# One GNN layer pair on one core: the factor pieces on ScalarE's queue, the destination rows behind the table stores, the order test ahead of the node scales

## The chip, the cores and the metric

The kernel runs on one core of one Trainium2 chip. Time is device microseconds of that core. The kernel before takes 2129.64 us (median of three runs, 2129.09 to 2132.87). The execution that the profiler recorded took 2125.4 us by its own clock, of which the profile's span covers 2123.5 us.

## The reference

6250 nodes with 512 features each, 100000 edges sorted by destination. Two Chebyshev graph convolutions stand around a layer norm, ahead of them a layer norm with ReLU, and at the end the input is added again:

```python
deg  = segment_sum(ones(E), src, N)
dinv = where(deg > 0, rsqrt(maximum(deg, 1.0)), 0.0)
norm = -dinv[src] * dinv[dst]

def prop(h):                       # one sum over the edges of each node
    return segment_sum(h[src] * norm[:, None], dst, N)
def cheb_conv(h, W0, W1, b):
    return h @ W0 + prop(h) @ W1 + b

h = relu(layernorm(x))
h = cheb_conv(h, W1_0, W1_1, b1)
h = layer_norm(h, gamma, beta)
h = where(h >= 0, h, 0.01 * h)
out = x + cheb_conv(h, W2_0, W2_1, b2)
```

## The kernel before, in words

The work has a setup and two layers.

**Setup.** SyncE's queue (SP in the profile) loads the edge sources and then all of x into `arena`, as 125 partitions of 50 nodes each, in eleven groups of tiles, every group in a piece of 112 and one of 13 partitions (L339). ScalarE (ACT) makes sum, squares and ReLU of most tiles (L536 to L555), VectorE (DVE) those of eight tiles. VectorE also builds one-hot tiles of the edge sources (L787) and TensorE (PE) multiplies them into a histogram, which is the degree of every node (L1107). The normalized rows go to a table in HBM, `table[0]`, whose rows have 516 elements: 512 features and behind them a factor of the node (four elements, 16 bytes, of which the first is used). SP stores the features, group by group, in twenty DMAs (L359, semaphore `s_tab`, shown as table0_out). The factor needs the degrees, so it is ready last: VectorE's reciprocal at L832 raises `s_factor`. It is stored in three pieces, each a DMA of as many 16-byte runs as it has nodes: 48 partitions from ScalarE's queue (L574, 2400 runs), 64 and 13 partitions from SP's (L363, 3200 and 650 runs). All three raise `s_factor_out` (row_factors_out).

**Edges.** The edges are cut into 782 columns of 128, called slots, and 53 chunks of 14 or 15 slots; a chunk sums into 128 nodes from a base. For that the kernel needs the source index of every slot (`idx_all`) and its destination (`dst_rows`, turned into `loc_all`). SP loads both as rows (`slot_rows`, L343 to L347, three DMAs each) ahead of the table stores; TensorE turns them (`turn`, L1100). VectorE writes `idx_all` (L850), casts the destinations (L853), tests that the edges are sorted (`order`, L734 to L743), works out the chunks' bases (`bases`, L750 to L782, which raises `s_flag` and `s_base`), and makes `loc_all` ready (L861 to L883, `s_loc`). The scales of the nodes (L833 to L844, `s_scales`) stand ahead of all this, right behind the factor. SP stores them (L365), loads the first weights (L368, 2 MB) and then the first chunk's own rows and scales (L375, L377).

**Layers.** GpSimd (POOL) issues one indirect DMA per slot (L494), which gathers 128 rows of the table into one of 30 row buffers: 782 in each layer, 1564 in all. In layer 0 it has to wait for the whole table, `s_tab` and `s_factor_out`. ScalarE rounds a gathered row (L597, L598) into PSUM and SBUF, VectorE makes the remainder (L918, L922) and one-hot tiles (L892, L893), TensorE multiplies one-hots with rows (L1221 to L1230) and does the dense parts (L1093). A buffer is free when the slot is summed: GpSimd waits for `s_slot` of two chunks before, every five slots. Layer 1 does the same from `table[1]`, which layer 0 writes.

What sets the order around the change: each engine's program is written out by hand; a queue takes its DMAs in the order of the program. GpSimd's program waits for `idx_all`, the flag, the table and the factors, and then branches to `general` (edges not sorted) or `layer` (sorted, the case here):

```python
pool.wait_ge(s_idxr, 2)
pool.wait_ge(s_flag, 1)
bad = pool.value_load(flag_i[0:1, 0:1], min_val=0, max_val=1)
pool.wait_ge(s_tab, 2 * 16 * (NG - 1))
pool.wait_ge(s_factor_out, 48)
with pool.If(bad > 0):
```

Of the kernel before, what the change touches and what calls it, by code (L numbers as in the profile page):

```python
# [14 lines left out]
P = 128  # L15
# [18 lines left out]
def gnn_kernel(nc, x, src, dst, W10, W11, b1, gamma, beta, W20, W21, b2, out):  # L34
    N, D = x.shape
# [6 lines left out]
    TA = 112  # L42
    ACT_ROWS = 48

# [49 lines left out]
    with ctx:  # L94
# [234 lines left out]
        def _(sp):  # L329
# [21 lines left out]
            slot_rows(src, idx_all, s_idx)  # L351
            slot_rows(dst, dst_rows, s_dsts)
            for g in range(1, NG):
# [4 lines left out]
                for n0, n1 in parts:  # L358
                    sp.dma_start(table_rows[n0:n1, t0:t1, 0:D], nodes[n0:n1, t0:t1, :]).then_inc(s_tab, 16)  # L359
            sp.wait_ge(s_factor, 1)  # L360
            with nc.allow_non_contiguous_dma(reason="the factor in each row of the table"):
                for n0, n1 in ((ACT_ROWS, TA), (TA, TR)):
                    sp.dma_start(table_rows[n0:n1, :, D:RW], factors[n0:n1, :, :]).then_inc(s_factor_out, 16)  # L363
            sp.wait_ge(s_scales, 1)
# [89 lines left out]
        def _(pool):  # L454
# [9 lines left out]
            def general(L):  # L464
                if L == 1:
                    pool.wait_ge(s_gout, 16 * (NC + 1))
                with pool.Fori(0, NC) as i:
                    n = L * NC + i
# [15 lines left out]
            def layer(L):  # L484
                if L == 1:
                    pool.wait_ge(s_tab1, 16 * (NC + 1))
                for i in range(NC):
                    u = i % 2
# [12 lines left out]
            bad = pool.value_load(flag_i[0:1, 0:1], min_val=0, max_val=1)  # L501
            pool.wait_ge(s_tab, 2 * 16 * (NG - 1))
            pool.wait_ge(s_factor_out, 48)
            with pool.If(bad > 0):
# [7 lines left out]
        def _(act):  # L512
# [60 lines left out]
            with nc.allow_non_contiguous_dma(reason="the factor in each row of the table"):  # L573
                act.dma_start(table[0].rearrange("(p t) n -> p t n", t=NT)[0:ACT_ROWS, :, D:RW],  # L574
                              factors[0:ACT_ROWS, :, :]).then_inc(s_factor_out, 16)

# [115 lines left out]
        def _(dve):  # L692
# [117 lines left out]
            for t in range(HT):  # L810
# [7 lines left out]
                if mine is not None:  # L818
# [12 lines left out]
            dve.wait_ge(s_sqvdeg, 1)  # L831
            nc.vector.reciprocal(factors[:, :, 0], sqrt_veps_deg).then_inc(s_factor, 1)  # L832
            post.add(nc.vector.tensor_scalar(hasdeg, hist_ps[0:TR, 0:NT], 0.0, None, ALU.is_gt))  # L833
            dve.wait_ge(s_sqdeg, 2)
# [12 lines left out]


            dve.wait_ge(s_idxps, 1)
            nc.vector.tensor_copy(idx_all[:, 0:4 * P], src_ps[0][:, :]).then_inc(s_idxr, 1)  # L850
            nc.vector.tensor_copy(idx_all[:, 4 * P:S], src_ps[1][:, 0:S - 4 * P]).then_inc(s_idxr, 1)
            dve.wait_ge(s_dsts, 48)
            nc.vector.tensor_copy(dst_rows_f[:, 0:FB * P], dst_rows[:, 0:FB * P]).then_inc(s_dstrows, 1)  # L853
            nc.vector.tensor_copy(dst_rows_f[0:S - FB * P, FB * P:],
                                  dst_rows[0:S - FB * P, FB * P:]).then_inc(s_dstrows, 1)

            order()
            bases()

# [225 lines left out]
        def _(pe):  # L1085
# [11 lines left out]
            def turn(to, source):  # L1097
                for b in range(FB + 1):
                    n = min(P, S - b * P)
                    last = nc.tensor.transpose(to[b // 4][:, b % 4 * P:b % 4 * P + n], source[0:n, b * P:(b + 1) * P],  # L1100
                                               ident[0:n, 0:n])
                return last
# [10 lines left out]
            with pe.Fori(0, HT // 2) as k:  # L1113
# [8 lines left out]

            pe.wait_ge(s_dstrows, 2)
            turn(dst_ps, dst_rows_f).then_inc(s_locps, 1)
            pe.wait_ge(s_viol, 1)
# [3 lines left out]
            nc.tensor.matmul(misc_ps[:, 192:192 + NC], ones_row[:, :], chunk_f[:, 0, :], start=True,  # L1129
                             stop=True).then_inc(s_basesum, 1)  # L1130
            pe.wait_ge(s_flag, 1)
            bad = pe.value_load(flag_i[0:1, 0:1], min_val=0, max_val=1)
# [162 lines left out]
```

## Time and profile before

| | |
|---|---|
| median of three runs | 2129.64 us (2129.09 to 2132.87) |
| the profiled execution | 2125.4 us |
| its span | 2123.5 us |
| first gather starts | 113.58 us |
| gathers | 1564 |
| PE busy | 1900.1 us (89%) |
| ACT busy | 1509.1 us (71%) |
| POOL busy | 1487.0 us (70%) |
| DVE busy | 1457.6 us (69%) |

The busy shares are averages over the whole span. GpSimd's 70% leaves out the time between two of its instructions, which is not counted as busy. The setup is the first 113.6 us; ScalarE works without a gap in it until 94.9 us, and the DMA engines are busy until about 107 us. "SPq" and "ACTq" rows are the DMA instructions of those queues: their duration is the time that the issuing engine needs to hand over the DMA, not the transfer.

### The profile page before, as it was taken

How to read it: one execution, taken by the hardware profiler on the slowest of the kernel's cores; microseconds unless marked ns; L12 is line 12 of the kernel's file. 1: busy time of each engine (PE TensorE's matmuls, PEld its weight loads, DVE VectorE, ACT ScalarE, POOL GpSimd, SP SyncE). 2: the span in 40 equal slices, each digit the busy share in tenths (PEclk: the TensorE clock that was granted, in tenths of full speed). 3: DMA queues.
4: the chain of work that ended last, by engine and by line, in shares of the span. 5: the costliest groups of instructions: out<-in, count | busy, mean ns of one | idle time of the engine just before them, and what ended most of it. 6: DMA issues, size and time to landing. Idle time of an engine off the chain costs nothing.

```text
span 2123.5 us, 25622 instructions
## 1 busy us (share of the span) xinstructions
PE 1900.1 (89%) x6702; PEld 1067.5 (50%) x6702; DVE 1457.6 (69%) x3379; ACT 1509.1 (71%) x2720; POOL 1487.0 (70%) x1574
## 2 busy tenths in 40 slices
PE   3459999999999999999996999999999999999998
PEld 3325555555555555555543555555555555555554
DVE  9948777777777777777765555556565655666653
ACT  7757777778777777787755666666666666666664
POOL 0067777777777777777746777777777777777774
PEclk9979999999999999999997999999999999999999
DMA  9998888888888888888856888888888888888885
GB/s 230 284 297 241 239 239 242 241 241 238 242 242 241 238 241 242 241 236 242 241 149 217 250 255 255 254 246 254 252 250 255 254 255 251 252 253 246 256 254 158
DMA packets 195466, 515.61 MB, mean 243 GB/s; under 512 B 44312, under 2 KB 45999, under 8 KB 195325
## 3 DMA queue, kind: packets, MB, share of 16 engines
q0 software_dynamic: 125120, 411.69, 65.9%
q1 hardware_dynamic: 67376, 101.91, 15.3%
q8 instruction: 50, 0.82, 0.2%
q10 hardware_dynamic: 2828, 0.44, 0.1%
q14 instruction: 92, 0.75, 0.1%
HBM read 473.08 MB, written 40.84 MB: 242 GB/s over the span
## 4 chain that ended last, share of the span: by engine, by line
POOL 33%; PE 22%; issue 15%; ACT 13%; DMA 11%; DVE 5%; SPq 0%; ACTq 0%; POOLq 0%; DVEq 0%
POOL arena L494 33%; PE ps L1093 12%; DMA arena<-table,idx_all 10%; PE ps L1230 5%; ACT ps L597 3%; ACT high L597 3%; PE ps L1223 2%; PE ps L1221 2%; DVE low L918 1%; ACT hots_full L549 1%; ACT high L598 1%; ACT arena L630 1%; ACT arena L536 1%; ACT arena L555 1%; DVE ps L1000 1%
## 5 line engine op out<-in xcount | busy, mean ns | idle before, releaser
L494 POOL DMA_INDIRECT arena<-table,idx_all x1564 | 1483.2, 948 | 549.7 <-issue 499.6
L922 DVE TENSOR_TENSOR low<-arena,ps 128x512 fp32r<-128x512 f32 x517 | 353.4, 686 | 391.6 <-ACT ps L598 378.8
L1221 PE MATMUL ps<-high,hots 128*128 128x512 f32 x1034 | 569.8, 551 | 4.6 <-ACT high L597 2.4
L1230 PE MATMUL ps<-arena,hots_full 128*128 128x512 f32 x1060 | 544.6, 596 | 0.4 <-DMA arena<-table,idx_all 0.4
L918 DVE SCALAR_TENSOR_TENSOR low<-arena,ps 128x512 fp32r<-128x512 f32 x517 | 385.8, 747 | 209.8 <-ACT ps L597 177.8
L598 ACT CAST ps<-arena 128x512 fp32r<-128x512 f32 x517 | 304.3, 589 | 315.0 <-DMA arena<-table,idx_all 307.6
L1223 PE MATMUL ps<-low,hots 128*128 128x512 f32 x1034 | 408.4, 395 | 0.0
L597 ACT ACTIVATE ps<-arena 128x512 fp32r<-128x512 f32 x517 | 354.3, 685 | 45.3 <-DMA arena<-table,idx_all 45.1
L597 ACT ACTIVATE high<-arena 128x512 fp32r<-128x512 f32 x517 | 369.6, 715 | 0.0
L598 ACT CAST high<-arena 128x512 fp32r<-128x512 f32 x517 | 317.8, 615 | 1.4 <-PE ps L1223 1.4
L892 DVE TENSOR_SCALAR hots<-iota_f,loc_all 128x128 fp32r<-128x128 f32 x1034 | 264.8, 303 | 9.8 <-PE ps L1223 6.1
L1221 PEld LDWEIGHTS ps<-high,hots 128*128 128x128 f32 x1034 | 196.9, 190 | 132.6 <-issue 78.1
L1223 PEld LDWEIGHTS ps<-low,hots 128*128 128x128 f32 x1034 | 196.8, 190 | 121.6 <-issue 72.7
L1093 PE MATMUL ps<-arena 128*128 128x512 f32 x424 | 204.0, 626 | 57.3 <-ACT arena L630 57.3
L1230 PEld LDWEIGHTS ps<-arena,hots_full 128*128 128x128 f32 x1060 | 185.1, 191 | 69.8 <-issue 50.2
L1093 PE MATMUL ps<-w_all,arena 128*128 128x512 f32 x424 | 196.0, 605 | 24.4 <-ACT arena L630 24.4
L1088 PE MATMUL ps<-ident,arena 128*128 128x128 f32 x848 | 131.1, 278 | 69.5 <-ACT arena L620 40.5
L1093 PE MATMUL ps<-w_all,work 128*128 128x512 f32 x424 | 190.6, 592 | 0.0
L1093 PE MATMUL ps<-arena,work 128*128 128x512 f32 x424 | 190.6, 592 | 0.0
L1088 PEld LDWEIGHTS ps<-ident,arena 128*128 128x128 f32 x848 | 102.3, 141 | 154.5 <-ACT arena L620 87.4
L1093 PEld LDWEIGHTS ps<-arena 128*128 128x128 f32 x424 | 80.1, 197 | 159.2 <-issue 81.6
L1093 PEld LDWEIGHTS ps<-w_all,arena 128*128 128x128 f32 x424 | 76.4, 190 | 123.0 <-issue 76.0
(133 smaller groups left out, 1330.9 us busy)
## 6 DMA issues: line engine op xcount, KB each, us to landing
arena<-table SPq DMA_DIRECT2D x106, 256.0 KB, 3.7
arena<-table,idx_all POOLq DMA_INDIRECT x1564, 3.9
table<-arena SPq DMA_DIRECT2D x53, 256.0 KB, 4.0
arena<-in_x_dram SPq DMA_DIRECT2D x53, 256.0 KB, 6.0
out_dram<-arena SPq DMA_DIRECT2D x53, 256.0 KB, 3.9
table<-arena SPq DMA_DIRECT2D x10, 1120.0 KB
arena<-in_x_dram SPq DMA_DIRECT2D x9, 1120.0 KB
w_all<-in_L_gnn_W_dram SPq DMA_DIRECT2D x2, 1024.0 KB, 9.9
```

The costliest lines, as they stand in the source:

```text
L494: nc.gpsimd.indirect_dma_start(out=rows[u][:, c, 0:RW if L == 0 else D], out_offset=None, in_=table[L][:, :], in_offset=bass.IndirectOffse ...
L536: last = nc.scalar.activation(nodes[:, t, :], nodes[:, t, :], ACT.Copy, accum_out=col(row_sum, t))
L597: return nc.scalar.activation(to, rows[u][:, c, 0:D], ACT.Copy, scale=rows[u][:, c, D:D + 1])
L598: return nc.scalar.copy(to, rows[u][:, c, 0:D])
L892: return nc.vector.tensor_scalar(hot_of(u, c), iota_f[:, :], loc, None, ALU.is_equal)
L918: nc.vector.scalar_tensor_tensor(out=low[a], in0=rows[u][:, c, 0:D], scalar=rows[u][:, c, D:D + 1], in1=high_ps[s % NB][:, :], op0=ALU.mul ...
L922: nc.vector.tensor_tensor(low[a], rows[u][:, c, 0:D], high_ps[s % NB][:, :], ALU.subtract).then_inc(s_low, 1)
L1088: last = nc.tensor.transpose(to[:, k * P:(k + 1) * P], source[:, k * P:(k + 1) * P], ident[:, :])
L1093: last = nc.tensor.matmul(to[:, :], source[:, k * P:(k + 1) * P], w[:, k, :], start=start and k == 0, stop=stop and k == KC - 1)
L1221: nc.tensor.matmul(tx_ps[u][:, :], hot, high[a], start=c == 0, stop=False)
L1223: last = nc.tensor.matmul(tx_ps[u][:, :], hot, low[a], start=False, stop=i == NC - 2 and c == SLOTS - 1)
L1230: last = nc.tensor.matmul(tx_ps[u][:, :], hot, rows[u][:, c, 0:D], start=c == 0, stop=i == NC - 2 and c == SLOTS - 1)
```

## The change

Five edits. (1) ScalarE's queue stores all of the factor, in two pieces of 112 and 13 partitions; SP stores none, and the constant ACT_ROWS goes. (2) SP loads the destination rows behind the last table store and no longer ahead of the first. (3) On VectorE the cast of `idx_all`, `order` and `bases` stand right behind the factor, and the node scales behind these. (4) TensorE turns the destination rows behind the two small matmuls of the order test and the bases. (5) GpSimd waits for the table and the factors behind its branch, at the head of layer 0, and the sum that it waits for is 32 instead of 48, since there are two pieces.

```diff
--- before.py
+++ after.py
@@ -40,7 +40,6 @@
     TR = 125
     NT = N // TR
     TA = 112
-    ACT_ROWS = 48
 
     XG = (0, 2) + tuple(range(5, NT + 1, 5))
     NG = len(XG) - 1
@@ -349,7 +348,6 @@
 
             sp.wait_ge(s_setup, 3)
             slot_rows(src, idx_all, s_idx)
-            slot_rows(dst, dst_rows, s_dsts)
             for g in range(1, NG):
                 t0, t1 = XG[g] if g > 1 else 0, XG[g + 1]
                 sp.wait_ge(s_ha, sum(t not in DVE_TILES for t in range(t1)))
@@ -357,10 +355,7 @@
                     sp.wait_ge(s_hd, sum(t in DVE_TILES for t in range(t1)))
                 for n0, n1 in parts:
                     sp.dma_start(table_rows[n0:n1, t0:t1, 0:D], nodes[n0:n1, t0:t1, :]).then_inc(s_tab, 16)
-            sp.wait_ge(s_factor, 1)
-            with nc.allow_non_contiguous_dma(reason="the factor in each row of the table"):
-                for n0, n1 in ((ACT_ROWS, TA), (TA, TR)):
-                    sp.dma_start(table_rows[n0:n1, :, D:RW], factors[n0:n1, :, :]).then_inc(s_factor_out, 16)
+            slot_rows(dst, dst_rows, s_dsts)
             sp.wait_ge(s_scales, 1)
             sp.dma_start(node_scales.rearrange("(p t) c -> p (t c)", t=NT),
                          scal_all[:, :, :].rearrange("p t c -> p (t c)")).then_inc(s_scal_out, 16)
@@ -464,6 +459,9 @@
             def general(L):
                 if L == 1:
                     pool.wait_ge(s_gout, 16 * (NC + 1))
+                else:
+                    pool.wait_ge(s_tab, 2 * 16 * (NG - 1))
+                    pool.wait_ge(s_factor_out, 32)
                 with pool.Fori(0, NC) as i:
                     n = L * NC + i
                     with pool.Fori(0, EC) as e:
@@ -484,6 +482,9 @@
             def layer(L):
                 if L == 1:
                     pool.wait_ge(s_tab1, 16 * (NC + 1))
+                else:
+                    pool.wait_ge(s_tab, 2 * 16 * (NG - 1))
+                    pool.wait_ge(s_factor_out, 32)
                 for i in range(NC):
                     u = i % 2
                     for c in range(slots_of(i)):
@@ -499,8 +500,6 @@
             pool.wait_ge(s_idxr, 2)
             pool.wait_ge(s_flag, 1)
             bad = pool.value_load(flag_i[0:1, 0:1], min_val=0, max_val=1)
-            pool.wait_ge(s_tab, 2 * 16 * (NG - 1))
-            pool.wait_ge(s_factor_out, 48)
             with pool.If(bad > 0):
                 general(0)
                 general(1)
@@ -571,8 +570,9 @@
             nc.scalar.activation(row_std, row_veps, ACT.Sqrt).then_inc(s_sqdeg, 1)
             act.wait_ge(s_factor, 1)
             with nc.allow_non_contiguous_dma(reason="the factor in each row of the table"):
-                act.dma_start(table[0].rearrange("(p t) n -> p t n", t=NT)[0:ACT_ROWS, :, D:RW],
-                              factors[0:ACT_ROWS, :, :]).then_inc(s_factor_out, 16)
+                for n0, n1 in ((0, TA), (TA, TR)):
+                    act.dma_start(table[0].rearrange("(p t) n -> p t n", t=NT)[n0:n1, :, D:RW],
+                                  factors[n0:n1, :, :]).then_inc(s_factor_out, 16)
 
             def general(L):
                 with act.Fori(0, NC) as i:
@@ -830,6 +830,13 @@
             nc.vector.tensor_scalar_max(deg1, hist_ps[0:TR, 0:NT], 1.0).then_inc(s_deg1, 1)
             dve.wait_ge(s_sqvdeg, 1)
             nc.vector.reciprocal(factors[:, :, 0], sqrt_veps_deg).then_inc(s_factor, 1)
+
+            dve.wait_ge(s_idxps, 1)
+            nc.vector.tensor_copy(idx_all[:, 0:4 * P], src_ps[0][:, :]).then_inc(s_idxr, 1)
+            nc.vector.tensor_copy(idx_all[:, 4 * P:S], src_ps[1][:, 0:S - 4 * P]).then_inc(s_idxr, 1)
+            order()
+            bases()
+
             post.add(nc.vector.tensor_scalar(hasdeg, hist_ps[0:TR, 0:NT], 0.0, None, ALU.is_gt))
             dve.wait_ge(s_sqdeg, 2)
             post.add(nc.vector.reciprocal(dinv, sqdeg))
@@ -845,17 +852,10 @@
             post.settle(dve)
             dve.sem_inc(s_scales, 1)
 
-
-            dve.wait_ge(s_idxps, 1)
-            nc.vector.tensor_copy(idx_all[:, 0:4 * P], src_ps[0][:, :]).then_inc(s_idxr, 1)
-            nc.vector.tensor_copy(idx_all[:, 4 * P:S], src_ps[1][:, 0:S - 4 * P]).then_inc(s_idxr, 1)
             dve.wait_ge(s_dsts, 48)
             nc.vector.tensor_copy(dst_rows_f[:, 0:FB * P], dst_rows[:, 0:FB * P]).then_inc(s_dstrows, 1)
             nc.vector.tensor_copy(dst_rows_f[0:S - FB * P, FB * P:],
                                   dst_rows[0:S - FB * P, FB * P:]).then_inc(s_dstrows, 1)
-
-            order()
-            bases()
 
             dve.wait_ge(s_locps, 1)
             post.add(nc.vector.tensor_copy(loc_all[:, 0:4 * P], dst_ps[0][:, :]))
@@ -1120,14 +1120,14 @@
             nc.tensor.matmul(hist_ps[:, 0:NT], zeros_b[:, 0:P], zeros_b[:, 0:NT], start=False,
                              stop=True).then_inc(s_histend, 1)
 
-            pe.wait_ge(s_dstrows, 2)
-            turn(dst_ps, dst_rows_f).then_inc(s_locps, 1)
             pe.wait_ge(s_viol, 1)
             nc.tensor.matmul(misc_ps[0:1, 128:129], viol[:, 0:1], ones[0:EP, 0:1], start=True,
                              stop=True).then_inc(s_violsum, 1)
             pe.wait_ge(s_base, 1)
             nc.tensor.matmul(misc_ps[:, 192:192 + NC], ones_row[:, :], chunk_f[:, 0, :], start=True,
                              stop=True).then_inc(s_basesum, 1)
+            pe.wait_ge(s_dstrows, 2)
+            turn(dst_ps, dst_rows_f).then_inc(s_locps, 1)
             pe.wait_ge(s_flag, 1)
             bad = pe.value_load(flag_i[0:1, 0:1], min_val=0, max_val=1)
 
```

SP's queue from the last table store on. Before (`dst_rows` had been loaded ahead of the first table store, L343 to L347):

```order
L359 DMA table<-arena 13x5x512
L363 DMA table<-factors 3200x1x4
L363 DMA table<-factors 650x1x4
L365 DMA node_scales<-scal_all 125x300
L368 DMA w_all<-in_L_gnn_W_0_dram 128x4x512
L368 DMA w_all<-in_L_gnn_W_1_dram 128x4x512
L444 TENSOR_LOAD flag_i
```

And now, in the same place:

```order
L357 DMA table<-arena 13x5x512
L342 DMA dst_rows<-in_dst_dram 128x6x128
L344 DMA dst_rows<-in_dst_dram 13x128
L346 DMA dst_rows<-in_dst_dram 1x32
L360 DMA node_scales<-scal_all 125x300
L363 DMA w_all<-in_L_gnn_W_0_dram 128x4x512
L363 DMA w_all<-in_L_gnn_W_1_dram 128x4x512
L439 TENSOR_LOAD flag_i
```

The two factor DMAs have left the queue, and the three loads of the destination rows stand where they stood.

VectorE right behind the factor (the reciprocal into `factors`). Before:

```order
L832 RECIPROCAL factors<-node_vec 125x50
L833 TENSOR_SCALAR node_vec<-ps 125x50
L835 RECIPROCAL scal_all<-node_vec 125x50
L836 RECIPROCAL scal_all<-node_vec 125x50
L837 COPY scal_all<-node_vec 125x50
L839 SCALAR_TENSOR_TENSOR node_vec<-scal_all,node_vec 125x50
L841 TENSOR_SCALAR scal_all<-scal_all 125x50
L843 TENSOR_TENSOR scal_all<-node_vec 125x50
L844 TENSOR_TENSOR scal_all<-node_vec,scal_all 125x50
L850 CAST idx_all<-ps 128x512
L851 CAST idx_all<-ps 128x270
L853 CAST work<-dst_rows 128x768
```

And now:

```order
L832 RECIPROCAL factors<-node_vec 125x50
L835 CAST idx_all<-ps 128x512
L836 CAST idx_all<-ps 128x270
L734 CAST dst_f<-dst_f 125x800
L736 CAST viol<-nxt_i 125x1
```

The eight operations of the node scales have moved behind `bases` (behind L782), and the casts of `dst_rows` behind them.

## Rows read from the trace of the kernel before

**Rows 1.** Page, parts 4 and 5: chain by engine; the gathers

```profile
POOL 33%; PE 22%; issue 15%; ACT 13%; DMA 11%; DVE 5%; SPq 0%; ACTq 0%; POOLq 0%; DVEq 0%
...
L494 POOL DMA_INDIRECT arena<-table,idx_all x1564 | 1483.2, 948 | 549.7 <-issue 499.6
```

**Rows 2.** Instructions of L494: first and last start, idle time by releaser

```profile
L494 POOL DMA_INDIRECT arena<-table,idx_all x1564: 940/946/1132, 113.6 to 2099.8; - x196
...
  DMA table<-arena: 28.1, 1
```

**Rows 3.** Waits of POOL, 113 to 1100 us: total, times, longest

```profile
POOL arena L494 <- PE ps L1230: 3.4, 11, 0.3
POOL arena L494 <- PE ps L1223: 1.2, 4, 0.3
```

**Rows 4.** Chain of waits, 92 to 125 us: start, us, what

```profile
94.87 1.69 SPq L359
...
96.61 3.09 SPq L359
...
99.74 2.09 SPq L363
...
101.89 10.51 DMA table<-factors
...
112.69 0.89 issue
113.58 1.13 POOL arena L494
```

**Rows 5.** Chain of waits, 1112 to 1130 us: the first gather of layer 1

```profile
1118.92 2.06 DMA table<-arena
1120.98 0.26 issue
```

**Rows 6.** Timeline of SP, 47 to 61 us: start, us, operation

```profile
56.12 3.78 SPq L345 DMA_DIRECT2D dst_rows<-in_dst_dram  x1
```

**Rows 7.** Busy time by stretch; the last three columns are PEclk, DMA share, GB/s

```profile
61.00:94.60 33.60, 16.23 (x328) 14.62 (x328) 32.19 (x34) 33.60 (x87) 3.07 (x2) 1.00 1.03 319
...
107.00:108.00 1.00, 0.00 (x0) 0.00 (x0) 0.21 (x2) 0.00 (x0) 0.00 (x0) 0.50 0.81 11
108.00:112.00 4.00, 0.00 (x0) 0.00 (x0) 1.85 (x9) 0.00 (x0) 0.00 (x0) 0.50 0.56 42
```

**Rows 8.** DMA queues, 97 to 102 us (q1 SP's, q10 ACT's): packets, MB

```profile
q1 hardware_dynamic: 580, 1.13, 80.5%
q10 hardware_dynamic: 1354, 0.02, 14.6%
```

**Rows 9.** DMA queues, 101 to 102 us

```profile
q10 hardware_dynamic: 481, 0.01, 26.8%
```

**Rows 10.** DMA queues, 102 to 107 us

```profile
q10 hardware_dynamic: 1051, 0.02, 12.2%
```

**Rows 11.** DMA packets of all queues, 106 to 107 us

```profile
DMA packets 1229, 0.06 MB, mean 62 GB/s; under 512 B 1208, under 2 KB 1208, under 8 KB 1229
```

**Rows 12.** Timeline, 60 to 175 us (the part up to 109 us)

```profile
95.52 0.74 ACTq L574 DMA_DIRECT2D table<-factors  x1
...
98.19 0.55 DVE L853 CAST work<-dst_rows 128x768 f32<-128x768 int32 x1
...
108.15 0.65 SPq L365 DMA_DIRECT2D node_scales<-scal_all  x1
```

**Rows 13.** Timeline, 106 to 124 us

```profile
101.89 6.22 SPq L363 DMA_DIRECT2D table<-factors  x1
...
108.86 1.85 DVE L892 TENSOR_SCALAR hots<-iota_f,loc_all 128x128 fp32r<-128x128 f32 x9 [1.62 <-issue]
...
120.03 0.69 ACT L597 ACTIVATE ps<-arena 128x512 fp32r<-128x512 f32 x1 [24.78 <-DMA arena<-table,idx_all]
...
122.72 1.09 PE L1088 MATMUL ps<-ident,arena 128*128 128x128 f32 x4 [17.88 <-DMA scal<-node_scales]
```

## The prediction

> **What bounds the kernel now.** I start with the page: its chain gives GpSimd the largest share, 33%, and in the list of groups the gathers have 1564 instructions of 948 ns, with 499.6 us of their idle time put to "issue" and not to another engine [rows 1]. The reader is to see that a gather costs its 0.95 us and about 0.30 us between two. So I ask for the gathers alone: they run from 113.6 to 2099.8 us, and one wait breaks the row, 28.1 us for the table of layer 1 [rows 2]. 1564 x 1.25 = 1955, plus 28.1, is 1983 of the 1986 us between first and last start. Nothing else is left to explain. The waits of GpSimd in layer 0 say the same: for TensorE it waits 4.6 us in all, never over 0.3 us [rows 3]. The kernel is a GpSimd program of fixed length: whenever its first gather starts, the last starts 1986 us later. TensorE's 89% busy is no bound here.
>
> So the whole question is when the first gather starts. The chain from 92 us on [rows 4] gives what it stands on. SP hands over the last table stores (94.87, 96.61), then a factor piece (99.74), then the last, the 650-run piece, at 101.89. The handing over of that piece alone takes 6.22 us, until 108.11 [rows 13], so the chain's "DMA table<-factors" of 10.51 us ends at 112.40 and consists of 6.22 us in which the queue did not take the piece and 4.29 us from there to its landing. Then come three small sequencer steps and 0.89 us of "issue", and the gather starts at 113.58 [rows 4]: 1.18 us behind the landing.
>
> **The change, part by part.**
>
> *GpSimd's wait behind the branch.* Now nothing but the gather stands behind the wait. The same situation is in the trace once: at the start of layer 1 the table's last store lands at 1120.98 and the gather follows 0.26 us later [rows 5]. Gain: 1.18 - 0.26 = 0.92 us. Bounds: 0 (if the 0.89 us belong to the first gather and not to the branch) and 1.0.
>
> *Destination rows behind the table stores.* They are 100000 x 4 B = 0.40 MB. At the 319 GB/s of the stretch of the table stores [rows 7] that is 1.25 us of all DMA engines taken from in front of the tables. Handing them over took 3.78 us for the middle one [rows 6], which is the queue being full and not a cost of its own. Can the tables use it? SP hands over the last group at 94.87, as soon as ScalarE is ready with it [rows 4]; that moment does not move, but behind it the queue is shorter by these 1.25 us. The table stores end at about 107 us, since in the microsecond behind that the core moves 11 GB/s [rows 7]; I take 105.7. But the 0.40 MB now go in the same stretch as the factor, on the other queue, and take back 1.25 us at the most from it. Net for the first gather: between 0 and -1.25, I take 0 and leave the gain as part of the packing below.
>
> *The factor on one queue.* 6250 runs of 16 bytes. ScalarE's piece of 2400 was handed over at 95.52 in 0.74 us [rows 12]. From 97 to 102 us its queue moved 1354 packets beside 580 of SP's [rows 8], 481 of them in the last microsecond [rows 9], and from 102 to 107 us the other 1051 [rows 10], then with SP's own 16-byte runs as rivals. When the big packets are gone the engines do 1208 small ones in a microsecond [rows 11]. From this:
> - by 102 us: 1354, as before.
> - 102 to 105.7 us, beside the last table stores, at the 481 per us of rows 9: 1780. Sum 3134.
> - left: 3116, beside the destination rows. At 1208 per us that is 2.6 us, plus 1.25 us for the 0.40 MB: 109.6 us.
> - the second piece (650) must then still land. Before, 4.29 us passed from its acceptance to the landing; it then had 3200 runs ahead of it, now 5600. If it is taken while the last 1500 or so of the first piece are still under way (some 1.5 us before their end), it lands at 109.6 - 1.5 + 4.3 = 112.4; if it flows right behind them and only the last write has to be confirmed (2.06 us from issue to landing for a whole store at the start of layer 1 [rows 5]), at 109.6 + 1.3 = 110.9. I take 112.0, near the end that goes by the 4.29 us row.
>
> Then 112.0 + 0.26 = 112.3 us for the first gather, against 113.58: 1.3 us earlier. The ends of this term: all packets perfectly packed (below) give 108.7; the mean rate of rows 8, 271 per us, for all 5600 runs gives 97 + 20.7 + 4.3 = 122.0.
>
> On this the Trainium skill has a rule that speaks against the edit: the page "DMA: Bandwidth & Descriptors", section "Issuing engines are not separate DMA queues", says that transfers from any engine run on the same 16 DMA engines and interleave, so that another queue saves only the issuing time. This trace agrees in part: the DMA share is already at 1.03 in the stretch of the table stores [rows 7], but in the four microseconds before the factor landed it is 0.56 [rows 7], and there it is the handing over that is late. By the rule alone the edit would gain nothing.
>
> *VectorE.* The flag needs `order` and `bases`; they now stand some 1.7 us earlier, and GpSimd has long waited for other things: no gain, no cost. The node scales come later, by the length of `order` and `bases`; the casts of the destination rows are at 98.19 and all of this was done long before SP asked for the scales at 108.15 [rows 12]. Their new end is about 95.5 + 1.1 + 5.5 + 1.8 = 104 us, an estimate from the lengths in the timeline. SP, behind the destination rows, arrives at 105 or later: nothing.
>
> *The destination rows late.* They land at about 109, not 66. The cast, the turn and the rest to `s_loc` took from 98.19 to about 107.2; without `order` and `bases` in between it is about 6 us: 115. The first one-hot tiles come 1.62 + 1.85 us behind [rows 13]: 118.6. ScalarE, which waits for `s_loc` too, began with the first row at 120.03, TensorE at 122.72, when the first own rows and scales were there [rows 13]. So this is hidden, by 4 us, if the destination rows land by 113. Behind it stands another cover: GpSimd needs nothing from TensorE before its 30th gather, 29 x 1.25 = 36 us after the first. Price if the first cover goes: 0 for GpSimd still; if both go, microsecond for microsecond.
>
> **Sum.** 1.3 us earlier and all else equal: 2125.4 - 1.3 = 2124.1 us for a profiled execution (span 2123.5 - 1.3 = 2122.2). The median of the runs stands 4.2 us above the profiled execution, so 2129.64 - 1.3 = 2128.3 us. About 0.2%, 4.3 us, is what a measurement of this kernel can tell from no change.
>
> **The rivals.**
>
> *Good packing (faster).* From 95 us to the landing the DMA engines have the same work as before less their gaps. The gaps were 4 x 0.44 + 0.19 = 1.95 us [rows 7], and the destination rows' 1.25 us have gone from in front if the factor gets ahead of them. If the small piece does not tail, 112.40 - 1.95 - 1.25 - 0.8 (the last 0.8 being the smaller part of the 4.29 us that no packets fill) = 108.4, first gather 108.7, 4.9 us earlier: 2124.7 us. For it: ScalarE's queue has nothing else in it, and 481 small packets passed in the last microsecond [rows 9], where SP's queue does 116 big ones on average [rows 8]. A rule of the Trainium skill would bring it about ("DMA: Bandwidth & Descriptors", section "Queues, rings and completion order": an engine goes round between the queues by whole packets, which can hold many descriptors). The trace agrees so far that four 16-byte runs passed for each big packet at 101 us. Against it: the small piece's 4.29 us, and that the mean over 97 to 102 us was only 2.3 to 1 [rows 8].
>
> *The queue starves (slower).* The factor now needs one queue for all 6250 runs, and SP's queue is refilled behind the tables with destination rows, node scales and 2 MB of weights; before, the weights came behind the factor in the same queue. If ScalarE's queue keeps only the 271 per us of rows 8, its first piece ends at 117.7 and the second lands at 122.0: first gather 122.3, 8.7 us later, 2138.3 us. With 350 per us it is 97 + 16 + 4.3 = 117.3 and 2133.6 us. It is slower than before from the point where the landing is behind 113.3, and visibly so from 117.6, which is a mean rate below 344 per us. Against it: 1208 per us once the tables are done [rows 11].
>
> *The tail is the same (no change).* The small piece is taken only when the big one is through, and that is at 108 us again: landing 112.4, gain 0.9 us by the branch alone, 2128.7 us. It lies within my forecast's range.
>
> *The start does not reach the end (no change).* The consumers take over as the bound for the microseconds won, for instance by the late `s_loc`: 2129.6 us. Against it: GpSimd's waits for TensorE are 0.3 us at the most [rows 3].
>
> **How the numbers follow.** Forecast with its twin (a first gather at 111.0 to 113.4): 0.52, its own range 2127 to 2129.5 us. Good packing: 0.26. Starving queue: 0.14. Start lost: 0.08. Visible at 0.2% is a gain from a first gather before 109.3, a bit over half of the good-packing case: faster 0.15. Half of the starving case is beyond +4.3 us: slower 0.07. The rest is 0.78. The range of 8 in 10 takes in most of the good packing and the milder half of the starving case: 2124.3 to 2132.8 us.
>
> **What would show it.** In the profile after: (a) the first gather's start, and all gathers behind it at 1.25 us, so that the span moves by the same amount; (b) "issue" between the factor's landing and the gather at 0.3 instead of 1.18 us; (c) the handing over of ScalarE's second piece, and the packets of its queue per microsecond between 102 and 112 us; (d) no store of SP's later than about 106 us; (e) TensorE's first transposes at about 122 us. I am wrong if the first gather is before 109.5 or behind 114, or if it moves and the end does not.

## The result, and the profile after

The changed kernel takes 2139.48 us (median of 20 runs, 2130.78 to 2146.14), the kernel before 2128.85 us (20 runs, 2125.64 to 2132.87). The ratio is 1.0046, 95% interval 1.0036 to 1.0056: about 10 us slower, outside the range I gave. The profiled execution after took 2146.14 us (span 2144.3), the slowest of its 20, and that of before, 2125.4 us, lies below all of the 20 (2125.64 and up), so the two traces show twice the median's difference; a second profile of the changed kernel (e17 below) shows 2133.56 us. In e5 to e16 (called the long rounds below), on three chips of which one is that of e1 to e4, every kernel, the one before too, took 16 to 19% longer (before: 2464.89, 2527.00 and 2531.59 us); of those the ratio to before and the setup's part of the trace are used.

Where the time went is in the chain of waits of the changed kernel, 92 to 140 us (start, us, what), which answers to [rows 4]:

```profile
97.39 0.75 ACTq L574
...
98.18 32.60 DMA table<-factors
...
130.82 0.89 issue
131.71 1.13 POOL arena L495
```

The factor lands at 130.78 and no longer at 112.40; the first gather starts at 131.71, 18.13 us later than before. Behind it all is as it was. The gathers (line 495 now) and what ended GpSimd's idle time, which answers to [rows 2]:

```profile
L495 POOL DMA_INDIRECT arena<-table,idx_all x1564: 940/946/1131, 131.7 to 2118.7; - x196
...
  DMA table<-factors: 60.6, 1
  DMA table<-arena: 28.3, 1
```

From first to last gather it is 1987 us, before 1986. The span grew by 20.8 us: 18.1 before the first gather, 0.8 between the gathers, 1.9 behind the last.

What happens between 98 and 131 us is in the packets. SP's queue and ScalarE's of the changed kernel, 102 to 107 us, then 115 to 122 us (packets, MB, share of 16 engines' time), to be held against [rows 8, 10, 11]:

```profile
q1 hardware_dynamic: 393, 0.77, 85.6%
q10 hardware_dynamic: 1589, 0.03, 31.5%
```

```profile
q1 hardware_dynamic: 852, 1.67, 91.1%
q10 hardware_dynamic: 237, 0.00, 2.2%
```

In the seven microseconds from 115 on ScalarE's queue moves 34 packets per us. They take 2.2% of 112 us of engine time, 10 ns each: the runs themselves are short, the time passes between them. SP's queue has the engines, 852 packets in 91.1%, which is 120 ns each. Those are its weights, 2 KB a packet, handed over at 108.42. SP's timeline, 95 to 125 us, shows when they were handed over:

```profile
102.03 2.24 SPq L342 DMA_DIRECT2D dst_rows<-in_dst_dram  x1
104.31 2.22 SPq L344 DMA_DIRECT2D dst_rows<-in_dst_dram  x1
...
107.43 0.94 SPq L360 DMA_DIRECT2D node_scales<-scal_all  x1
108.42 2.61 SPq L363 DMA_DIRECT2D w_all<-in_L_gnn_W_dram  x2
```

And ScalarE's line in its own timeline, 96 to 126 us:

```profile
97.39 26.62 ACTq L574 DMA_DIRECT2D table<-factors  x2
```

The first piece was handed over in 0.75 us, so the second took 25.84 us, until 124.02. Then it needs 6.76 us more to land.

The consumers were ready before the first gathered row. VectorE's cast of the destination rows comes at 117.13, TensorE's first transposes at 125.42, ScalarE's first row at 135.27, after a wait for the gather (timeline, 94 to 142 us):

```profile
117.13 0.56 DVE L856 CAST work<-dst_rows 128x768 f32<-128x768 int32 x1 [11.96 <-DMA dst_rows<-in_dst_dram]
...
125.42 1.09 PE L1088 MATMUL ps<-ident,arena 128*128 128x128 f32 x4 [5.80 <-DMA scal<-node_scales]
...
135.27 0.69 ACT L597 ACTIVATE ps<-arena 128x512 fp32r<-128x512 f32 x1 [38.14 <-DMA arena<-table,idx_all]
```

### The profile page after: what moved, and what is told of

It is laid out like the page before. It is cut to its first block, busy times and chain, and to the rows that moved or that the text cites. A ratio compares the mean times of both kernels' runs of the same rounds, so it can differ in the third digit from the quotient of the medians.

```text
span 2144.3 us, 25621 instructions
## 1 busy us (share of the span) xinstructions
PE 1905.4 (89%) x6702; PEld 1068.8 (50%) x6702; DVE 1456.8 (68%) x3379; ACT 1509.6 (70%) x2720; POOL 1486.5 (69%) x1574
## 4 chain that ended last, share of the span: by engine, by line
POOL 35%; PE 24%; issue 15%; DMA 11%; ACT 7%; DVE 6%; SPq 0%; ACTq 0%; POOLq 0%; DVEq 0%
POOL arena L495 35%; PE ps L1093 12%; DMA arena<-table,idx_all 9%; PE ps L1230 6%; PE ps L1223 2%; PE ps L1221 2%; ACT ps L597 2%; ACT high L597 2%; DMA table<-factors 2%; DVE w_all L787 1%; ACT high L598 1%; DMA arena<-in_x_dram 1%; PE ps L1088 1%; DVE low L918 1%; ACT arena L630 1%
## 5 line engine op out<-in xcount | busy, mean ns | idle before, releaser
L1223 PEld LDWEIGHTS ps<-low,hots 128*128 128x128 f32 x1034 | 196.5, 190 | 122.7 <-issue 76.7
L1088 PEld LDWEIGHTS ps<-ident,arena 128*128 128x128 f32 x848 | 102.6, 141 | 140.8 <-ACT arena L620 85.8
```

The costliest lines, as they stand in the source:

```text
L1088: last = nc.tensor.transpose(to[:, k * P:(k + 1) * P], source[:, k * P:(k + 1) * P], ident[:, :])
L1223: last = nc.tensor.matmul(tx_ps[u][:, :], hot, low[a], start=False, stop=i == NC - 2 and c == SLOTS - 1)
```

## The experiments

Theory Q: SP's queue, refilled behind the tables, starves ScalarE's. Its rivals: the destination rows in the same stretch (R), the queue slow by itself (T), the order of the two pieces.

### e1: the queue alone

```diff
 (the kernel before)
-            sp.wait_ge(s_factor, 1)
-            ... sp.dma_start(table_rows[n0:n1, :, D:RW], factors[n0:n1, :, :]) for 48..112, 112..125
-                act.dma_start(... [0:ACT_ROWS, :, D:RW], factors[0:ACT_ROWS, :, :])
+                for n0, n1 in ((0, TA), (TA, TR)):
+                    act.dma_start(... [n0:n1, :, D:RW], factors[n0:n1, :, :])
-            pool.wait_ge(s_factor_out, 48)
+            pool.wait_ge(s_factor_out, 32)
```

> The kernel before with the first edit alone: all of the factor on ScalarE's queue in two pieces, the destination rows still ahead of the table stores, waits and VectorE's order as before. Theory Q (the queue starves: SP's queue, refilled behind the tables with scales and weights, holds up the 16-byte runs of the other queue, and the second piece is not taken until the first is through): the loss is here. First gather at 122 us or later, handing over of the second piece over 15 us, time 2135 to 2145 us. Rival R (the loss comes from the destination rows, which now move in the same stretch as the factor): first gather at 112 to 115 us, time within 2 us of before.

Measured: 2139.26 us, ratio 1.0048 (1.0035 to 1.0061), first gather at 124.93, the second piece handed over in 20.90 us, all as theory Q said. The whole loss is in this edit; R is out as its cause. Chain of waits, 95 to 126 us:

```profile
95.77 0.75 ACTq L570
...
96.56 27.20 DMA table<-factors
```

Here the weights come at once behind the tables (SP hands them over from 99.00 on), and ScalarE's queue moves 452 packets between 107 and 112 us beside 579 of SP's:

```profile
q1 hardware_dynamic: 579, 1.11, 93.3%
q10 hardware_dynamic: 452, 0.01, 10.7%
```

### e2: all but the queue

```diff
 (the changed kernel)
+            sp.wait_ge(s_factor, 1)
+            ... sp.dma_start(table_rows[n0:n1, :, D:RW], factors[n0:n1, :, :]) for 48..112, 112..125
             slot_rows(dst, dst_rows, s_dsts)
             (ScalarE stores 0..48; GpSimd waits for 48)
```

> The changed kernel with the first edit undone: the factor in three pieces as before (48 partitions on ScalarE's queue, 64 and 13 on SP's behind the tables), the destination rows behind them. Theory Q: the loss is gone. First gather at 111 to 113.5 us, time 0 to 2.5 us below before. Rival R: the rows beside the tail of the factor still cost, first gather behind 118 us, time 5 us or more above before.

Measured: 2127.21 us, ratio 0.9989 (0.9980 to 0.9998): a gain of about 2 us, as theory Q says. Chain, 97 to 114 us:

```profile
97.17 2.84 SPq L362
...
100.06 11.72 DMA table<-factors
```

The small piece on SP's queue was taken at 108.34 (100.06 and 8.28 us of handing over) and landed at 111.78; first gather at 112.71. So the other four edits are worth a little, or at least nothing is lost by them.

### e3: scales and weights held back

```diff
 (the changed kernel)
             slot_rows(dst, dst_rows, s_dsts)
+            sp.wait_ge(s_factor_out, 32)
             sp.wait_ge(s_scales, 1)
```

> The changed kernel, but SP waits for both factor pieces before it stores the node scales and loads the 2 MB of weights. Theory Q, if the weights are what starves the queue: the first piece ends soon after the tables and the destination rows, first gather at 117 to 121 us, so at least 10 us before that of the changed kernel's profile; time 2130 to 2134 us. Rival T (the queue is slow by itself, or the tables alone hold it up): first gather still at 125 us or later, time as the changed kernel's.

Measured: 2129.08 us, ratio 0.9996 (0.9987 to 1.0006). One wait on SP, with both factor pieces still on ScalarE's queue, takes the loss away, more than I expected. Chain, 94 to 114 us, then the queues from 102 to 107 us and from 107 to 112 us:

```profile
96.88 14.94 DMA table<-factors
```

```profile
q10 hardware_dynamic: 2963, 0.05, 65.1%
q1 hardware_dynamic: 779, 0.52, 64.1%
```

```profile
q10 hardware_dynamic: 1966, 0.03, 23.2%
q1 hardware_dynamic: 132, 0.06, 4.2%
```

The factor lands at 111.82 and the first gather starts at 112.75. From 102 to 107 us the queue moves 2963 runs where the changed kernel's first profile has 1589, but that is not the weights' doing: there they were not yet handed over (108.42), and the second profile of the changed kernel (e17) has 2830 in the same five microseconds, with the weights handed over from 104.00 on. The wait shows behind that. The changed kernel in e17, 107 to 112 us, then 112 to 120 us:

```profile
q1 hardware_dynamic: 498, 0.73, 77.0%
q10 hardware_dynamic: 1318, 0.02, 38.7%
```

```profile
q1 hardware_dynamic: 1403, 2.17, 83.2%
q10 hardware_dynamic: 1016, 0.02, 7.2%
```

With the weights held back everything is through by 111.82; beside them the last thousand runs take another eight microseconds. T is out: the queue is fast enough when no weights stand in SP's. The wait also holds back all that stands behind the weights in SP's program, the first chunk's rows and the layer's constants, so it is "the weights and what follows them" that e3 has moved away.

### e13: the weights alone held back

```diff
 (the changed kernel)
+            sp.wait_ge(s_factor_out, 32)
             for k, w in enumerate((W10, W11)):
```

> The changed kernel, where SP stores the node scales as soon as it comes to them and waits for the factor only before the 2 MB of weights. If the weights starve the factor's queue: as with both held back, landed at 111 to 113 us and within 0.1% of before. If the node scales do: landed behind 118 us and 0.3% or more above before.

Measured, in a long round: ratio 0.9979 (0.9947 to 1.0012), factor landed at 114.67. That is 1.7 us behind what I expected if the weights are the cause, and before the 118 us that I gave for the scales; the small-first kernel of the same round (e14) has 1.0042 and 123.6 us. So it is the 2 MB of weights with what follows them; that the scales went ahead (handed over at once) did no harm that shows.

### e4: the branch alone

```diff
 (the kernel before: both waits moved from ahead of pool.If to the head of layer(0))
```

> The kernel before with the fifth edit alone: GpSimd waits for table and factor behind its branch. The prediction's term: 0.92 us earlier. The rival, after the changed kernel's profile, which still has 0.89 us of issue before the first gather: 0.2 to 0.3 us. Both lie below what five rounds can tell; the profile decides, by the time from the factor's landing to the first gather (0.26 or 0.93, against 1.18 before).

Measured: 2129.52 us, ratio 1.0005 (0.9996 to 1.0013). Chain, 104 to 118 us:

```profile
104.28 10.53 DMA table<-factors
...
114.85 0.89 issue
115.74 1.13 POOL arena L500
```

From the landing at 114.81 to the gather it is 0.93 us, as in the changed kernel. The edit is worth 0.25 us, not 0.92. (That the factor landed later here than in the profile of before, with nothing changed up to then, shows how far one profile differs from the next: 2.4 us.)

### e5, e9, e14, e17, e18: the order of the two pieces

```diff
 (the changed kernel)
-                for n0, n1 in ((0, TA), (TA, TR)):
+                for n0, n1 in ((TA, TR), (0, TA)):
```

> The changed kernel with the order of the two factor pieces on ScalarE's queue turned round: the 13 partitions first, then the 112. In the changed kernel the second piece is taken at 124.0 us and lands at 130.8. Theory Q1 (two delays in a row: the last DMA engines crawl through their share of the big piece until about 124 us, and only then the small piece is taken and runs): with the small one first only the crawl is left; factor landed at 120 to 126 us, time 2 to 7 us below the changed kernel. Rival Q2 (the last engine's share decides, whatever the order of pieces): no difference to the changed kernel beyond 2 us.

> The changed kernel with the small factor piece first, once more, since in the round before every kernel, the one before the change too, took about 16% longer from about 116 us on. There the factor landed at 121.9 us, with the second piece taken at 98.7 and not at 124.0. Where GpSimd alone is the bound the time should be 2135 to 2139 us: 2 to 6 us below the changed kernel, 6 to 10 above before. If the order of the pieces is nothing: 2139 us and more.

> The changed kernel with the small factor piece first. Its two profiles had the factor landed at 121.9 and 120.4 us, against 130.8 and 123.8 with the big piece first. With GpSimd as the bound that is 2135 to 2139 us, 7 to 10 us above before. If the piece order is nothing: as the changed kernel, 2139 us or more.

> The changed kernel itself, beside the one with the small piece first. Factor landed at 124 to 131 us, second piece taken behind 115 us; 0.3 to 0.6% above before.

> The small factor piece first. If the second delay is a part of the loss: factor landed 3 to 9 us before that of the changed kernel beside it, and 2 to 7 us (0.1 to 0.3%) less time. If the order is nothing: within 0.1% of the changed kernel.

The first three, all in long rounds: ratios 1.0046 (1.0024 to 1.0068), 1.0044 (1.0013 to 1.0075), 1.0042 (1.0013 to 1.0072). So the changed kernel (e17) and this one (e18) were run side by side: 2137.30 us, ratio 1.0044 (1.0027 to 1.0060), and 2135.66 us, ratio 1.0033 (1.0020 to 1.0046). Chains of e17 and of e18, 94 to 135 us:

```profile
96.61 23.76 DMA table<-factors
...
120.41 0.89 issue
```

```profile
96.73 25.92 DMA table<-factors
...
122.69 0.89 issue
```

With the small piece first the second piece is taken in 2 us instead of 19 to 26, and the factor lands at 121.9, 120.4, 123.6 and 122.7 us; with the big one first at 130.8, 123.8 (e1) and 120.4. My theory of two delays in a row is not borne out: the long handing over goes, and the landing stays (e18's is 2.3 us behind that of e17, not 3 to 9 us ahead). In either order it is the last few hundred runs that are slow: 146 packets of ScalarE's queue in e17 from 112 to 115 us, 74 in e18. That these are the runs of a few DMA engines that are behind the others is my guess; the traces do not tell a packet's engine. The 1.6 us of time between e17 and e18 lie within the intervals. The changed kernel's own landing at 120.4 us in e17 is a miss too: I had expected 124 to 131.

### e6, e10, e15: the destination rows held back too

```diff
 (the changed kernel)
+            sp.wait_ge(s_factor_out, 32)
             slot_rows(dst, dst_rows, s_dsts)
```

> The changed kernel, but SP waits for both factor pieces already before the loads of the destination rows, so that ScalarE's queue has only the table stores beside it. If the rows held the factor up as well as the weights do, the factor lands 1.5 to 3 us before that of the kernel that held back only scales and weights (111.8 us), and the rows come at about 113 us. If only the weights matter: landed at 111 to 112 us again. As GpSimd alone is the bound the late rows cost nothing in either case, unless the one-hot tiles come behind 36 us after the first gather; rival C (the consumers then are late and it shows at the end): time over 2 us above what the first gather says.

> The changed kernel with SP waiting for the factor before destination rows, scales and weights, once more. There the factor landed at 109.4 us and the first gather started at 110.3. Where GpSimd is the bound: 2125 to 2127.5 us, 2 to 4 us below before. If the late destination rows (landed at 113) hold up the consumers so that it shows at the end: at or above before.

> The changed kernel with SP waiting for the factor before destination rows, scales and weights. Its two profiles had the factor landed at 109.4 and 115.4 us. With GpSimd as the bound: 2125 to 2129 us, and not slower than before; if the rows beside the factor cost nothing, the same as the kernel that held back scales and weights (2129.1).

All three in long rounds: ratios 0.9993 (0.9974 to 1.0012), 0.9952 (0.9924 to 0.9981), 0.9951 (0.9914 to 0.9989). The factor landed at 109.4, 115.4 and 111.2 us, against 111.8 in e3. Whether the rows beside the factor cost anything is not settled by that. Two of the three ratios are below 1 by more than their interval, but in these rounds GpSimd is not the only bound (in e7 it waits 172.4 us for TensorE, up to 7.2 at a time, against 21.9 us, never over 0.3, in the kernel before), and what they are worth where it is was not measured. In all three, and in e12 and e16, the chain from 94 to 130 us goes by the node scales and the first chunk's load of them, not by a gather: what is held back here becomes the next thing that is waited for.

### e7, e11, e12, e16, e8: the small piece on ScalarE's queue; both repairs

```diff
 (e7, e11: as e2, but)
-                for n0, n1 in ((ACT_ROWS, TA), (TA, TR)):      # SP
+                for n0, n1 in ((ACT_ROWS, TA),):               # SP
+                for n0, n1 in ((0, ACT_ROWS), (TA, TR)):       # ScalarE
 (e12, e16: and sp.wait_ge(s_factor_out, 48) ahead of slot_rows(dst, ...))
 (e8: the small piece first, and e3's wait)
```

> All edits but the first, with one more: the factor in three pieces as before, but the small one (13 partitions) goes on ScalarE's queue behind the 48 partitions instead of on SP's behind the 64. In the kernel with only the first edit undone, SP's small piece was not taken until 108.3 us and landed at 111.8. If the handing over is what is late: landed at 108 to 110 us, first gather at 109 to 111, time 3 to 6 us below before. If ScalarE's queue holds the small piece just as long: landed at 111 to 113 us, time within 2.5 us below before.

> Factor in three pieces, 48 and 13 partitions on ScalarE's queue, 64 on SP's, all other edits in, once more. There the factor landed at 110.7 us. Where GpSimd is the bound: 2125.5 to 2128 us, 1.5 to 4 us below before, and within 2 us of the kernel with only the first edit undone (2127.2).

> As the last one, and SP holds destination rows, scales and weights until all three factor pieces have landed. If what is queued behind the factor is all that slows its tail: landed at 107.5 to 109.5 us, first gather 108.5 to 110.5, time 3 to 5 us below before (about 2125). If the tail is the queues' own: landed at 110 to 111.5, as without the wait.

> Factor in three pieces (48 and 13 partitions on ScalarE's queue, 64 on SP's), all other edits in, and SP waiting for the factor before rows, scales and weights. Best ratio of the round before (0.9945). With GpSimd as the bound: 2124 to 2127 us, 3 to 5 us below before; if the holding back is given back by late rows or weights: 2127 to 2129 us.

> The changed kernel with both repairs: the small piece first, and SP holds scales and weights until the factor has landed. With one repair alone the second piece was taken at 109.3 us and landed at 111.8. Theory Q1: without the second piece's 2.5 us, landed at 109 to 110.5 us, first gather at 110 to 111.5, time 2 to 4 us below before. Rival Q2: as with the hold alone, 2128 to 2130 us.

All in long rounds. e7 and e11: 0.9992 (0.9975 to 1.0009), 0.9988 (0.9959 to 1.0018), landed at 110.7 and 114.9, neither at the 108 to 110 that I had expected if the handing over alone were late. e12 and e16, the same kernel: 0.9945 (0.9910 to 0.9980), 0.9994 (0.9964 to 1.0024), landed at 111.9 and 112.6, behind both of my ranges; so half a per cent in such a round is no evidence. e8: 0.9984 (0.9965 to 1.0003), landed at 113.0, no sooner than with e3's wait alone (111.8), which is the second time that turning the order round wins nothing. None of them is slower than before, none is shown faster than e2, and e2 is the only one with a gain shown where GpSimd is the bound.

## Why the prediction was wrong, point by point

**The bound: right.** GpSimd's gathers are a row of fixed length. Behind the first gather the span is 2009.9 us before and 2012.6 after, and 2010.1 to 2013.5 in e1 to e4, e17 and e18. Each of these spans follows its first gather within 4 us.

**The step that failed: the factor on one queue.** The prediction let the last 3116 runs go at 1208 per us from 105.7 us on, beside nothing but the destination rows. It left out that SP's queue has more behind the rows. I had put SP at 105 us or later with the scales in hand, so the sum's own times let the weights go in right behind, in the microseconds in which I let the factor run free; I named them only in the rival. What the traces of the changed kernel show in its place: by 107 us 2613 (first profile) and 3945 (e17) packets of ScalarE's queue since 97, then 259 and 264 per us to 112 us, and behind that a tail, 34 per us from 115 to 122 us in the first profile, 49 per us from 112 to 115 in e17. The factor was predicted at 112.0; it lands at 130.8 and 120.4, in e1 at 123.8, and in e3, with the weights out of the way, at 111.8.

The second piece was to be taken with some 1500 runs of the first still under way. It is taken when all but 100 to 200 are through, in the changed kernel (124.02, 116.11) as in e3 (109.32). That 111.8 is so near to 112.0 is in part luck: in e3 the small piece needs 2.5 us from there and not 4.29. Two slips are small beside this: the 3116 runs contain the 650 that the next step adds again (0.5 us too much), and the four runs for each big packet "at 101 us" set 481 against the mean of five microseconds; in that microsecond SP's queue moves 95, so it was five.

**The rival that happened.** "The queue starves", to which I gave 0.14, has the right cause: SP's refilled queue. Its time, 2138.3 us against 2139.48, is nearer than its working deserves. It took a steady 271 runs per us. In e17 the queue is faster than that until 112 us, 351 per us, and then all but stops. No fixed number of runs per big packet describes this: it is 8 at 101 us in the changed kernel's first profile (849 beside 106), 1.4 from 104 to 107, and 0.28 from 115 to 122. So an estimate by the rates of [rows 8, 9] could have given the direction, and not the size.

The rule that I weighed from the Trainium skill was the right warning: the page "DMA: Bandwidth & Descriptors", section "Issuing engines are not separate DMA queues", says that another issuing engine gives no other DMA engines. The traces agree in so far as the two queues are in each other's way: from 107 to 112 us ScalarE's moves 1966 packets beside 132 of SP's (e3), and 1318 beside 498 (e17). But as I applied it, "gains nothing", it missed the loss. A second rule of that page, in "Queues, rings and completion order", is that an engine takes turns between queues, by whole packets. That alone does not explain the tail: if every DMA engine had runs waiting and took turns, at least one run would pass for each big packet, and 0.28 do. Either most engines had no runs left by then, or the turns are not even; no run here tells which, nor whether it is the engines or the memory behind them that the two queues contend for. That the weights cause the loss is shown by e1, e3 and e13; how they do it is open.

**What had hidden the price before.** In the kernel before, the weights stood in the same queue as the last 3850 runs, behind them. The order in SP's queue was a priority, and moving the runs to the other queue took it away (e1 has that edit alone, with the weights unchanged). e3 gives it back with a wait.

**Tables: later than forecast in one profile.** They were to land by 106 or so. In the changed kernel's first profile SP's queue still moves 167 packets of 2 KB between 107 and 108.4 us, before the weights are handed over; in e17 the smaller packets of the destination rows run before 107. They are not the last to come in the chain. From 104 to 107 us of the first profile:

```profile
q1 hardware_dynamic: 240, 0.48, 102.6%
q10 hardware_dynamic: 327, 0.01, 14.2%
```

240 packets in 102.6% of 48 us are 205 ns each, against 111 ns for the 580 of [rows 8]. The 16-byte runs beside them are not the reason: there are 109 per us of them here, 271 per us in [rows 8], and 631 per us in this profile from 102 to 104 us, where the big packets take 126 ns. What slowed them is open, and so is why this execution is some 10 us behind e17, the same kernel.

**The branch: wrong in size.** Forecast 0.92 us, measured 0.25. Layer 1's 0.26 us [rows 5] was the wrong model: 0.89 us of issue belong to the first gather of the program and stay with it.

**The small piece's tail: right that it is there, wrong as a term.** 4.26 us from acceptance (116.11) to landing in e17, as in [rows 4], but 2.5 us in e3 and 6.76 in the changed kernel's first profile, so it is no constant. And turning the order round won nothing that shows.

**VectorE, the late rows, the consumers: right.** The destination rows were cast at 117.1 (112.2 in e17) instead of about 109, and it cost nothing: GpSimd waits for TensorE 4.9 us in all in layer 0, never over 0.3 (before 4.6, [rows 3]):

```profile
POOL arena L495 <- PE ps L1230: 4.3, 14, 0.3
POOL arena L495 <- PE ps L1223: 0.6, 2, 0.3
```

**The scatter.** The changed kernel's 20 runs spread over 15.4 us, those of before over 7.2. The profiles point to the reason: in two executions of the same changed kernel the factor landed at 130.8 and at 120.4 us, beside the weights; that this makes the scatter of all 20 is not shown.

## What to carry to other kernels

When a transfer that something waits for is moved to another queue, list what stands behind it in its old queue: that order was its priority, and in the new queue it has none. Bytes do not say what many tiny runs need beside big packets. 100 KB of 16-byte runs needed 16 us from the first handing over to the landing with the 2 MB of weights held back (e3), and 25 to 33 us beside them (e17, the changed kernel's first profile), the difference being a slow tail; hold the big transfer back until the small one has landed, or keep both in one queue in the order in which they are needed.

## What was not expected of the hardware

The length of a 2 KB packet was not fixed: 205 ns at 104 to 107 us against 111 ns, with fewer 16-byte runs beside it. And the granted clock of TensorE between 96 and 110 us, where it hardly works, was not the same from one execution to the next. The kernel before (97 to 110 us) and e4, which is the same kernel up to GpSimd's branch (96 to 110 us; the sixth of the columns after the stretch is PEclk):

```profile
97.00:110.00 13.00, 2.61 (x11) 1.90 (x11) 10.82 (x46) 0.00 (x0) 0.00 (x0) 0.50 0.86 156
```

```profile
96.00:110.00 14.00, 2.61 (x11) 1.90 (x11) 11.26 (x48) 0.00 (x0) 0.00 (x0) 1.00 0.83 188
```

2.61 us of matmuls in both; 1.2 GHz in the one, 2.4 GHz in the other, and the seven transposes of the stretch (L1100 and L1104) take 1.75 and 1.76 us, so that the lower clock cost nothing that the profile shows. In the first TensorE's last matmul ended at 93.87, the clock fell at about 96.2, and the next came at 98.92; in the second it had nothing to do from 95.01 to 99.56, and the clock stayed. What makes the difference is open.
